# Another order of the same steps in a four-layer pipelined kernel, on TensorE, ScalarE, GpSimd and the DMA queue

## The reference

```python
x = _layernorm(x + _L0_attn_ref(x, W_q, W_kv, W_o))      # a: q, kv -> fft per head -> unit norm -> cumsum of kv -> product -> ifft -> W_o
x = _layernorm(x + _L0_ffn_ref(x, ...))                  # g: 8 experts' gates, argmax, rank-8 update, bias
x = _layernorm(x + _L1_attn_ref(x, W_qkv, W_o))          # b, e: 16-head softmax attention
x = _layernorm(x + _L1_ffn_ref(x, W_fc, W_proj))         # c: relu^2 MLP, hidden 1024, ternary weights, rms norm
```

## Time and profile before

| | |
|---|---|
| median of 3 runs | 836.21 us (835.87 to 844.2) |
| profiled execution | 837.45 us |
| its span, first to last instruction | 835.4 us |
| PE busy | 685.5 us, 82% of the span |
| DVE busy | 590.9 us, 71% |
| ACT busy | 477.9 us, 57% |
| POOL busy | 350.3 us, 42% |
| DMA moved | 60.57 MB, 73 GB/s over the span |
| granted TensorE clock, mean of the span | 0.904 |

### The profile page before, as it was taken

One profiled execution on the slowest core, in us unless ns is written; L12 is line 12 of the kernel. 1 busy time (PEld: TensorE's weight loads), 2 busy tenths in 40 slices (PEclk: granted clock), 3 DMA queues, 4 the chain that ended last, 5 costly groups with the idle time before them and its releaser, 6 DMA issues.

```text
span 835.4 us, 14806 instructions
## 1 busy us (share of the span) xinstructions
PE 685.5 (82%) x5100; PEld 542.5 (65%) x5100; DVE 590.9 (71%) x1429; ACT 477.9 (57%) x961; POOL 350.3 (42%) x537
## 2 busy tenths in 40 slices
PE   4354665878999999999999999999998988887673
PEld 3233453656677778787878787877786866755462
DVE  3766345858798888888888889898979685645020
ACT  0112113264858594959494958586767575673731
POOL 3302021120446463727282828273636343434544
PEclk9556558799999999999999999999999999999966
DMA  6100005262626253444434353525362516250000
GB/s 193 63 0 13 0 14 106 55 131 34 133 25 141 29 138 39 128 52 114 65 103 66 101 87 79 101 70 105 67 117 41 116 39 130 36 128 2 13 13 13
DMA packets 298170, 60.57 MB, mean 73 GB/s; under 512 B 237352, under 2 KB 293616, under 8 KB 298096
## 3 DMA queue, kind: packets, MB, share of 16 engines
q1 hardware_dynamic: 298096, 59.63, 34.9%
HBM read 38.38 MB, written 20.97 MB: 71 GB/s over the span
## 4 chain that ended last, share of the span: by engine, by line
DVE 40%; PE 38%; issue 8%; POOL 6%; ACT 4%; SPq 2%; DMA 1%; POOLq 0%; DVEq 0%; ACTq 0%
DVE nmax L1256 13%; PE pA L518 6%; PE pC L742 5%; PE pS L695 4%; PE pO L671 3%; DVE spec L1100 3%; DVE x L1061 3%; PE pA L603 2%; PE pA L502 2%; PE pA L538 2%; PE pA L565 2%; PE pC L720 2%; PE pS L645 2%; DVE y L1327 2%; DVE gt L1197 2%
## 5 line engine op out<-in xcount | busy, mean ns | idle before, releaser
L1256 DVE TENSOR_REDUCE nmax<-pB 128x2 f32<-128x512 f32 x256 | 168.4, 679 | 24.0 <-PE pB L619 23.8
L871 ACT ACTIVATE pt<-pS 128x512 f32<-128x512 f32 x256 | 148.6, 608 | 50.7 <-PE pS L645 48.9
L619 PE MATMUL pB<-kT,qT 96*128 96x256 bf16 x512 | 90.3, 279 | 15.1 <-DVE nmax L1256 13.6
L645 PE MATMUL pS<-qT,kT 98*128 98x256 bf16 x512 | 85.3, 276 | 10.4 <-ACT pt L871 6.2
L1454 POOL TENSOR_TENSOR hid_lo<-hh,hid 128x512 fp32r<-128x512 f32 x64 | 87.2, 1362 | 9.1 <-issue 7.8
L1431 POOL TENSOR_TENSOR hsum<-hsum,hsq 128x512 f32<-128x512 f32 x48 | 66.0, 1375 | 46.5 <-ACT hsq L911 45.7
L720 PE MATMUL pC<-x3T,w1T 128*128 128x256 f32 x256 | 72.4, 315 | 4.0 <-ACT hr L899 2.1
L671 PE MATMUL pO<-pt,v_ext 128*32 128x256 f32 x1024 | 68.9, 387 | 3.9 <-ACT pt L871 3.9
L619 PEld LDWEIGHTS pB<-kT,qT 96*128 96x128 bf16 x512 | 39.1, 99 | 47.2 <-DVE nmax L1256 35.6
L645 PEld LDWEIGHTS pS<-qT,kT 98*128 98x128 bf16 x512 | 42.6, 98 | 39.4 <-issue 18.4
L742 PE MATMUL pC<-w2T,hid 128*128 128x256 f32 x256 | 66.3, 299 | 0.3 <-DVE ms L1316 0.3
(11 more groups left out here) (175 smaller groups left out, 1827.4 us busy)
## 6 DMA issues: line engine op xcount, KB each, us to landing
qk_scratch<-qk_part SPq DMA_DIRECT2D x48, 256.0 KB, 4.8
qT<-qk_scratch SPq DMA_DIRECT2D x96, 128.0 KB, 2.8
kT<-qk_scratch SPq DMA_DIRECT2D x96, 128.0 KB, 2.7
xa<-in_x SPq DMA_DIRECT2D x16, 256.0 KB, 3.7
v_scratch<-qkv SPq DMA_DIRECT2D x16, 256.0 KB, 3.5
v_heads<-v_scratch SPq DMA_DIRECT2D x16, 256.0 KB, 3.0
out_y<-y SPq DMA_DIRECT2D x16, 256.0 KB, 3.1
pt<-in_wfc SPq DMA_DIRECT2D x1, 1024.0 KB, 7.6
```

The costliest lines, as they stand in the source:

```text
L619: ins = pe.matmul(pB[h % 2][:, s * T:(s + 1) * T], qT[k][0:STACK, u * P:(u + 1) * P], kT[k][0:STACK, h * T:(h + 1) * T], start=True, stop= ...
L645: ins = pe.matmul(pS[h % 2][:, s * T:(s + 1) * T], kT[k][:, u * P:(u + 1) * P], qT[k][:, h * T:(h + 1) * T], start=True, stop=True)
L871: act.activation(pt[:, (h // 4) % 2, h % 4].rearrange("p s n -> p (s n)"), pS[h % 2][:], ACT.Exp, scale=HD ** -0.5).then_inc(S["probs"], 1)
L1256: dve.tensor_reduce(nmax[:, h * SIDES:(h + 1) * SIDES], pB[h % 2][:].rearrange("p (s k) -> p s k", s=SIDES), AX.X, ALU.max, negate=True).t ...
```

## The change

No instruction and no wait is changed, only the table `ORDER`, and in it only the order of PE, ACT, POOL and SP; what stands at the cut between two turns, and the numbers that shift a step by a turn, follow from where each list begins. DVE has the same order before and after. From the diff, a line or two of the table (PE and SP):

```diff
-    "e_score_8:+1 g_x1t e_out_1:+1 e_score_9:+1 e_score_10:+1 g_gate b_max_0:+1 b_max_1:+1 e_score_11:+1 "
...
-    "g_out_2:+2 g_in_0:+2 w_load_fc:+1 w_load_proj:+1 w_load g_in_1:+2 g_in_2:+2 g_v_out:+2 p_load "
-    "g_v_in:+2 c_store:+2 g_out_0:+1 b_rows:+1 g_out_1:+1 "
+    "g_v_out:+4 w_load_fc:+3 c_store:+4 w_load_proj:+3 p_load:+2 g_v_in:+4 g_out_0:+3 b_rows:+3 w_load:+2 "
+    "g_out_1:+3 g_out_2:+3 g_in_0:+3 g_in_1:+3 g_in_2:+3 "
```

More of the change, by code:

```diff
@@ L127 @@
     "g_mean a_res1 a_bn a_mean a_norm1 "
[4 rows of a table removed]
+    "c_rms:+3 e_pow:+3 c_pow:+3 a_pow1:+2 g_pow2:+2 c_norm:+3 a_root_0:+1 a_root_1:+1 c_lo_0:+2 "
+    "a_root_2:+1 a_root_3:+1 a_root_4:+1 c_add_1:+2 c_lo_1:+2 c_add_2:+2 c_lo_2:+2 c_add_3:+2 c_lo_3:+2 "
+    "c_hsum:+2 "
+    "g_v_out:+4 w_load_fc:+3 c_store:+4 w_load_proj:+3 p_load:+2 g_v_in:+4 g_out_0:+3 b_rows:+3 w_load:+2 "
+    "g_out_1:+3 g_out_2:+3 g_in_0:+3 g_in_1:+3 g_in_2:+3 "
 ).split()
```

## The result

The changed kernel takes 848.7 us at the median of six runs (840.8 to 850.1), the kernel before 837.0. The ratio is 1.0112, with a 95% interval from 1.0058 to 1.0166: about 1% slower. The forecast was 836.3 us, within a range of 826 to 845. The distance between runs of one kernel mostly goes with TensorE's granted clock: the two changed runs with a mean of 0.91 took 840.8 and 843.6 us, the four with 0.894 to 0.898 took 847.8 to 850.1. So what follows is argued from full turns, which lie where PEclk is 9 in every slice, and from ratios; a difference of 2 or 3 us between two medians proves nothing here. The turn that holds it took 41.01 us, like the mean of all nine.

A forecast was written before the change was run, and what follows sets the result against it. A loop through SP's DMA issues was taken to set every full turn, with PE and DVE nearly full. 837.45 + 1.1 (eleven full turns) + 1 (filling) - 2 (draining) = 837.55, or 836.3 us by the median; range 826 to 845.

The forecast's parts named there:

- The ring: Loop from first `b_max` through maxima, `b_maxt_t`, `b_rows`, `g_out`, `g_in` to the next batch's `b_max`; sets the turn, 40.34 us at least.
- The size of the slack: Room between the last read's issue and `b_max_0`, beyond the 2.64 us PE must wait: 0.7 us a turn.
- jitter: Variation of the gap from last read's issue to `b_max_0`, 2.7 to 4.0 us; no longer absorbed, 0.05 us a turn added.
- `b_maxt_t` 0.75 us later: On PE behind `a_cum`, the step starts 0.75 us later a turn, delaying `b_rows` and all SP queues behind it.
- The gains of DVE: Shorter DVE waits at stage a's power (0.7), gate (0.6) and running sum (0.4), net 1.2 us a turn, turning into waits.
- The late x: Rival, chance 0.13: `p_load` behind `c_store` lands x late, PE waits 0.7 us a turn, 844 to 845 us.
- POOL against DVE: Rival, chance 0.12: POOL and DVE operations meet elsewhere and exclude each other, 0.6 us a turn longer, 843 us.
- Ring pushed back by `g_out_0`: Rival, chance 0.10: late `g_out_0` makes `b_rows` on SP 0.4 us longer each turn, +4.4 us, 842 us.
- Filling and draining: Turns at start and end: filling 1 us gained and 2 lost, +1; draining -2 as `e_vt` leaves the chain to `c_y`.

The follow-up runs named there:

- e3: Changed kernel with `e_score_9` and `e_score_10` back ahead of `b_max_0`; 840.8 us, ratio 1.0044 to the kernel before.
- e1: Changed kernel with `b_maxt_t` put back ahead of `a_cum` on PE; 840.2 us, ratio 1.0017 to the kernel before.
- e4: Changed kernel with `b_rows` issued from ACT's queue instead of SP's; 831.1 us, ratio 0.9914 to the kernel before.
- e6: Changed kernel with `b_rows` on ACT's queue and `b_maxt_t` back ahead of `a_cum`; 831.5 us, ratio 0.9930 to the kernel before.
- e9: e6 with `g_rest` on DVE moved behind the split of the maxima; 822.2 us, ratio 0.9819 to the kernel before.
- e10: Changed kernel with POOL's order of the kernel before; 848.4 us, ratio 1.0142 to the kernel before.
- e14: Changed kernel with only `p_load` back ahead of `c_store`; 841.9 us, ratio 1.0053 to the kernel before.
- e7: Kernel before with the changed kernel's POOL order alone; 845.9 us, ratio 1.0073 to the kernel before.
- e2: Kernel before with only `b_maxt_t` moved behind `a_cum` on PE; 847.2 us, ratio 1.0096 to the kernel before.
- e8: Kernel before with `b_rows` on ACT's queue and `b_maxt_t` behind `a_cum`; 839.9 us, ratio 1.0017 to the kernel before.

## Why the prediction was wrong

*What bounds the kernel.* Right in kind. The ring of the earlier trace rows is what the changed kernel runs on, and each of its stations is where the text put it: PE released by `kT` at `b_max_0`, new waits of DVE before the first L1257, an unchanged 15 us of issuing.

*The size of the slack, 3.3 - 2.64 = 0.7 us.* This step failed, and in the sum for a turn it weighs most: the sum "40.29 - 0.70 (slack) + 0.75" lets a later read use up all of it. The last stretch of the ring shrank by 0.36 us a turn, from 3.37 to 3.01, not by 0.70. For the kernel before, the 0.7 was a fair average: its last reads landed after 2.72 us in the mean, and `b_max_0` started 3.37 us behind their issue. The text had this from one turn, and called the 2.7 to 4.0 us of the others jitter of the ring, though the trace has the landing of every read, and those lie between 2.60 and 2.87. What it left out is that the landing does not stay the same when the read moves. In the changed kernel the last read met a q8 packet twice. The longer of the two:

```profile
467.25 0.61 SPq L422 DMA_DIRECT2D kT<-qk_scratch  x1
```

```profile
q8 instruction: 1, 0.02, 2.5%
kT<-qk_scratch SPq DMA_DIRECT2D x1, 128.0 KB, 4.6
```

```profile
471.91 0.54 PE L620 MATMUL pB<-kT,qT 96*128 96x256 bf16 x2 [2.03 <-DMA kT<-qk_scratch]
```

PE starts 4.66 us behind the issue. The mean landing rose by 0.25 us, to 2.97, and that is most of the slack that was not there. The whole sum for a turn, by the table: forecast +0.75 (`b_maxt_t`) - 0.70 (slack) + 0.05 (jitter) = +0.10; measured +1.00 (`b_maxt_t`) + 0.08 (issuing) - 0.36 (last stretch) = +0.72, the measured 0.73 but for rounding. So 0.29 of the 0.62 us that were missed are slack, 0.25 the later `b_maxt_t`, and 0.08 the issuing. That the prediction's sum with no slack at all gives 40.29 + 0.75 = 41.04, next to the measured 41.02, is luck.

*`b_maxt_t` 0.75 us later.* This term was too small. It came 22.29 us behind `b_max_0` in the turn shown, 0.93 later than before, and 1.00 on average of the nine. Its place behind `a_cum` was read rightly, 1.03 us behind that step's start (forecast 0.97). But `a_cum` itself gained only 0.20 us, not 0.39 (21.18 us behind `b_max_0` against 21.38), as PE reaches `a_proj_0` 0.17 us later than before. A sentence beside it was wrong, that the stretch up to `b_maxt_t` "is bound by DVE, whose order is unchanged": in the changed kernel DVE ends the split 0.35 us before `b_maxt_t` starts, so PE's order binds. And DVE is itself 0.97 us later there than before, for it now waits for PE at `rden`, 1.07 us a turn, a wait that before did not have. The transposes that release it (L683, `e_outt_1`) now stand behind `a_proj_0`; this is read from the order and not tested, but the scores inside the ring are not the reason, since e3 has the same 1.07. So even ahead of `a_cum` the step would have waited for DVE, and in e1 a part of the gain is DVE's earlier split (21.49).

*The gains of DVE.* The gate wait fell from 1.29 to 0.72 us (forecast 0.6 less), the wait for the sum went altogether (0.84, forecast 0.4), and that for `rsa` fell by 0.24 (forecast 0.7): POOL's own two steps, 0.22 us for the epsilon and 0.71 for the power, stand in what is left, 1.24 us, whatever goes ahead of them. As the prediction said, none of it reached the end; it turned into the waits of 12.2, 9.6 and 5.1 us above.

*The late x.* Not at work in the profile: PE waits for x in no full turn of the changed kernel. In e1, e4, e6, e9 and e10, which load x as late, it does in two turns each. For the changed kernel e14 leaves it open.

*POOL against DVE.* The mechanism is right, the place and size were not. L1198 of the earlier trace rows lost its stretch, and others gained one. DVE in nine turns of the changed kernel:

```profile
L1205 DVE TENSOR_TENSOR gt<-cst,gt 128x16 f32<-128x16 f32 x9 | 9.7, 1082 | 0.0
L1167 DVE TENSOR_TENSOR f<-f 128x128 f32<-128x128 f32 x9 | 7.3, 816 | 0.0
L1198 DVE TENSOR_TENSOR gt<-gt,cst 128x16 f32<-128x16 f32 x9 | 1.6, 176 | 0.3
L1199 DVE TENSOR_SCALAR two_less<-gt 128x2 f32<-128x2 f32 x9 | 1.5, 162 | 0.0
```

The first two had 120 and 300 ns before, the last two 1129 and 625. All in all DVE was busy for 34.78 us a turn before, 34.49 in the changed kernel, 35.51 in e7 and 33.54 in e4, for the same instructions. A spread of 2 us was priced at 0.6.

*Ring pushed back by `g_out_0`.* Did not happen: `b_rows` takes 1.20 us and is 0.66 us behind `b_maxt_t`, as before.

*Filling and draining.* Forecast +1 and -2, measured +2.7 and +1.6; the three turns between the nine and the draining part cost 1.8 more, 0.6 each. The first `b_max` of the fourth batch lies between 259.6 and 268.8 us over the kernels profiled here, and PEclk differs from one execution to the next in the slices of the filling part (one stretch of 20.5 us at a granted clock of 0.50 from 140.9 us in the changed kernel, 10.2 us from 145.3 before), so neither number can be laid to a step. The missing 2 us of gain in draining were claimed without a row, and no run shows them. Of the 12.5 us between the forecast for the profiled execution, 837.55, and its 850.02, the filling part has 1.7, the nine full turns 5.6 (6.5 against nine times 0.1), the three turns behind them 1.6 and the draining part 3.6. So the full turns are the larger part of the miss, and draining is second.

*The range.* It ended at 845 because every "slower" rival was priced alone. A slack of half the size (a full turn of 40.7) together with one of them lies at 845 to 848. Two small slips in the sums: the ring pushed back was added to 837.55, the others to 836.3, and comes to 840.7 and not 842 on the same footing; and the upper halves of the three slower rivals are 0.175 together, not 0.19. What was called ten full turns are nine, with ten reads.

## What to carry to other kernels

A gap between an issue and the start of its consumer is slack only as long as the transfer lands as early when it is moved. Read the landing of that transfer in every turn, not in one, and look for what it would run into if it went out later: here a packet of instructions that before stood just behind the read. If something stands there, let the forecast run from no slack to all of it. Where a loop passes through a queue that issues nearly without a pause, a step of 0.2 us ahead of the queue's first issue is worth most of the delay it is given (0.94 us of turn for 1.15 of delay in e2), while the same step costs nothing once a second queue has taken 1.2 us out of the loop (e8). And the order of a side engine that shares SBUF with DVE is not free to change: e7 moved nothing but POOL's steps and cost 0.7%.

## What the runs showed of the hardware

Between two turns of e9 the same DVE instruction, on operands of the same shape, took 0.16 and 1.20 us (L1195), or 0.67 and 1.68 us (L1102), by whether a POOL operation was running; the POOL operation behind L1101 of e7 grew from 1.28 to 1.72. The last of twelve reads of the same size and shape landed from 2.5 to 4.6 us behind its issue; the 18 of 192 that took 3.4 us or more were those in whose first 1.7 us a 16 KB packet of instructions had started on queue q8. Two DMA issues moved from SP's queue to ACT's occupied it for 1.20 us, as on SP, and ACT had a pause there. The mean granted clock of single executions lay between 0.89 and 0.92; e2's two executions at 0.899 took 850.8 and 851.2 us, those at 0.916 and 0.922 took 842.6 and 842.0. In the changed kernel 2.03 us of idle PE were followed by 3.4 us at a granted clock of 0.50.
